# New step orders on all five engines of a gated cross-attention block with routed FFN

## The reference

```python
def xattn(x, y):                                     # x: layernormed
    q = heads(x @ wq + bq); k = heads(y @ wk + bk); v = heads(y @ wv + bv)
    attn = softmax(einsum('bhqd,bhkd->bhqk', q, k) / sqrt(16))
    return merge(einsum('bhqk,bhkd->bhqd', attn, v)) @ wo + bo

def ffn(x):                                          # x: layernormed, 2048 x 256
    one_hot = onehot(argmax(softmax(x @ gate_w.T)), 2)
    h = relu(einsum('end,edh->enh', x[None] * one_hot.T[:, :, None], w1) + b1[:, None])
    expert_out = einsum('enh,ehd->end', h, w2) + b2[:, None]
    return expert_out.sum(0) + relu(x @ sw1 + sb1) @ sw2 + sb2

x = x + tanh(g_xattn) * xattn(layernorm(x), ctx)
x = x + tanh(g_ffn) * ffn(layernorm(x))
```

## Time and profile before

| | |
|---|---|
| runs | 337.96, 338.2, 340.09 us |
| median | 338.2 us |
| profiled execution | 339.18 us, of it span of the trace 337.4 us |
| TensorE busy | 317.1 us, 94% |
| VectorE, ScalarE, GpSimd busy | 232.3 (69%), 214.6 (64%), 186.2 (55%) us |

### The profile page before, as it was taken

One profiled execution on the slowest core, in us unless ns is written; L12 is line 12 of the kernel. 1 busy time (PEld: TensorE's weight loads), 2 busy tenths in 40 slices (PEclk: granted clock), 3 DMA queues, 4 the chain that ended last, 5 costly groups with the idle time before them and its releaser, 6 DMA issues.

```text
span 337.4 us, 7289 instructions
## 1 busy us (share of the span) xinstructions
PE 317.1 (94%) x2363; PEld 281.4 (83%) x2363; DVE 232.3 (69%) x517; ACT 214.6 (64%) x483; POOL 186.2 (55%) x261
## 2 busy tenths in 40 slices
...
GB/s 195 285 353 40 246 124 161 70 171 157 81 82 54 0 126 0 0 144 122 20 230 2 62 2 31 128 63 180 179 64 200 187 62 62 78 61 54 91 31 28
DMA packets 38151, 35.69 MB, mean 106 GB/s; under 512 B 16608, under 2 KB 35060, under 8 KB 37613
## 3 DMA queue, kind: packets, MB, share of 16 engines
...
...
## 4 chain that ended last, share of the span: by engine, by line
PE 64%; DVE 15%; ACT 7%; DMA 6%; issue 4%; POOL 1%; POOLq 1%; SPq 1%; ACTq 0%; DVEq 0%
PE y_ps L1545 24%; PE h_ps L1545 17%; PE bank L1545 9%; PE s_ps L1545 8%; DMA x_all<-in_x 5%; PE bank L1678 3%; DVE rsum L1267 2%; DVE smax L1249 2%; DVE probs L1261 1%; ACT probs L950 1%; DVE stats L1150 1%; ACT xn L901 1%; ACT pT L959 1%; DVE other_sum L1235 1%; PE bank L1782 1%
## 5 line engine op out<-in xcount | busy, mean ns | idle before, releaser
L693 POOL TENSOR_TENSOR probs<-probs,rinv 128x616 f32<-128x616 f32 x32 | 41.3, 1292 | 36.5 <-DVE rinv L1271 35.9
L1545 PE MATMUL y_ps<-sw,hT_hi 128*128 128x256 f32 x272 | 57.2, 291 | 1.2 <-DVE hT_lo L1523 1.2
L1545 PE MATMUL y_ps<-ew,hT_hi 128*128 128x256 f32 x256 | 54.6, 287 | 1.7 <-DVE hT_lo L1482 1.7
L1482 DVE TENSOR_TENSOR hT_lo<-h,hT_hi 128x256 fp32r<-128x256 f32 x64 | 28.9, 451 | 35.0 <-ACT h L1089 33.0
L1545 PEld LDWEIGHTS y_ps<-sw,hT_hi 128*128 128x128 f32 x272 | 44.9, 190 | 3.0 <-DVE hT_lo L1523 1.8
L1545 PEld LDWEIGHTS y_ps<-ew,hT_hi 128*128 128x128 f32 x256 | 42.7, 188 | 3.0 <-DVE hT_lo L1482 2.8
L1545 PE MATMUL h_ps<-x2T_hi,sw 128*128 128x512 f32 (+1 forms) x160 | 43.7, 359 | 0.0
L1086 ACT ACTIVATE hT_hi<-h_ps,vec_cols 128x256 fp32r<-128x256 f32 x32 | 15.2, 475 | 42.0 <-PE h_ps L1545 32.1
L998 ACT ACTIVATE hT_hi<-h_ps,vec_cols 128x512 fp32r<-128x512 f32 (+1 forms) x40 | 24.6, 614 | 22.5 <-PE h_ps L1545 18.0
L1545 PE MATMUL y_ps<-sw,hT_lo 128*128 128x256 f32 x136 | 38.4, 282 | 0.0
L1545 PE MATMUL y_ps<-ew,hT_lo 128*128 128x256 f32 x128 | 35.9, 281 | 0.0
...
## 6 DMA issues: line engine op xcount, KB each, us to landing
...
xs<-sorted_dram SPq DMA_DIRECT2D x8, 257.0 KB, 2.7
...
```

The costliest lines, as they stand in the source:

```text
L693: nc.gpsimd.tensor_tensor(pq, pq, rinv[:, b % 2, k, :].unsqueeze(2).to_broadcast([P, HG, KEYS]), ALU.mult).then_inc(p_ready, 1)
L1482: nc.vector.tensor_tensor(hT[1][:, c % HB, 0:RTOK], h32[:, c % 2, 0:RTOK], hT[0][:, c % HB, 0:RTOK], ALU.subtract).then_inc(h_lo, 1)
L1545: return nc.tensor.matmul(out_, lhsT, rhs, start=start, stop=stop, **kw)
```

## The change

Only the five tables change. Every step occurs as often as before, no function is touched, and each engine executes the same instructions in another order. After the change the line numbers are lower by one, as `PE_ORDER` is a line shorter. The digits for the banks are new as well. Of the diff the part of SP is short enough to be read as it is:

```diff
 SP_ORDER = """
-    fl.0 kw.0 vz.0 vz.1 kw.1 kr.1 kr.2 wd.0 vw.0 wd.1 vw.1 vr.0 kr.3 vw.2 vr.1 vr.2 kr.4 vw.3 wd.3 vw.4 vr.3
-    kr.5 vr.4 wd.2 vw.5 vw.6 vr.5 kr.6 vw.7 ps.0 kr.7 vr.6 vr.7 ps.1 wd.4 wd.5 ps.2 ps.3 xs
+    kw.0 kw.1 vz.0 vz.1 kr.1 wd.0 vw.0 wd.1 kr.2 vr.0 vw.1 kr.3 vr.1 vw.2 kr.4 wd.3 vr.2 vw.3 vr.3 kr.5 vw.4 kr.6
+    vr.4 wd.2 vw.5 kr.7 vr.5 vw.6 vw.7 vr.6 vr.7 wd.4 wd.5 ps.0 ps.1 xs ps.2 ps.3 fl.0
 """
```

More of the change, by code:

```diff
@@ L92 @@
[L92 to L96, removed]
+    warm.0 yt.0 yt.1 yt.2 yt.3 vt warm.1 kp.0.0 in.0.0 kp.0.1 kp.1.0 qy.0.0 kp.1.1 sc.0.0 in.1.1 vp.0 qy.1.1 vp.1
@@ new lines @@
+    ine.5.0 qe.4 ex.3.0 vae.1.1 te.2.0.0 te.2.1.0 xn2.0 q32.5.0 te.2.2.1 te.2.3.0 te.2.4.1 n2e.0.0.0 qe.5 ex.3.1
+    ex.3.2 vae.2.1 he.0 te.3.0.0 ex.3.3 nm.6 he.1 he.2 te.3.1.1 he.3 ine.6.0 ex.4.0 he.4 te.3.2.1 he.5 nm.7 te.3.3.0
+    te.3.4.1 he.6 ex.4.1 q32.6.0 ine.7.1 he.7 xn2.1 vae.3.0 n2e.1.0.1 ex.4.2 n2e.1.1.0 ex.4.3 he.8 qe.6 ex.5.0 he.9
+    he.10 he.11 te.4.0.1 te.4.1.0 te.4.2.0 te.4.3.1 he.12 te.4.4.0 ex.5.1 ex.5.2 q32.7.1 vae.4.0 he.13 ex.5.3
+    te.5.0.0 qe.7 ex.6.0 ex.6.1 te.5.1.0 he.14 te.5.2.1 te.5.3.1 te.5.4.1 he.15 ex.6.2 ex.6.3 xn2.2 vae.5.0
@@ L112 @@
+    n2e.2.0.1 ex.7.0 n2e.2.1.0 ex.7.1 te.6.0.1 te.6.1.0 he.16 he.17 te.6.2.1 te.6.3.1 ex.7.2 te.6.4.1 he.18 wh.2
+    he.19 vae.6.1 ex.7.3 te.7.0.1 te.7.1.0 he.20 wh.3 he.21 he.22 te.7.2.0 te.7.3.1 xn2.3 te.7.4.1 he.23 n2e.3.0.0
+    n2e.3.1.1 vae.7.0 he.24 he.25 he.26 he.27 wh.5 wh.4 he.28 he.29 xn2.4 n2e.4.0.0 he.30 he.31 he.32 he.33 he.34
+    he.35 he.36 he.37 othe.0 he.38 he.39 xse.1
 """
@@ new lines @@
+    r1.1.12 wolo sm.0.0 ss.0.0 inl.1.1 su.0.0 s1.2 s1.3 s1.4 s1.5 s1.6 s1.7 sd sm.0.1 ss.0.1 sm.0.2 su.0.1 sm.0.3
+    ss.0.3 su.0.2 sm.1.0 sm.1.1 inl.2.0 su.0.3 ss.1.1 su.1.0 su.1.1 sm.1.2 sm.1.3 ss.1.2 ss.1.3 inl.3.0 su.1.2
+    sm.2.0 ss.2.0 su.1.3 sm.2.1 su.2.0 ss.2.1 inl.4.1 val.0.0 sm.2.2 ss.2.2 x1.0.0 sm.2.3 su.2.1 wl.1 sm.3.0 s2.0
+    inl.5.0 su.2.2 su.2.3 val.1.1 sm.3.1 su.3.0 ss.3.1 x1.1.1 dg sm.3.2 ss.3.2 wl.0 n2l.0.0.0 su.3.1 su.3.2 sm.3.3
+    ss.3.3 val.2.1 sm.4.0 hl.0 su.3.3 x1.2.0 hl.2 inl.6.0 s2.1 hl.3 ch.0 sm.4.1 ss.4.1 su.4.0 sm.4.2 ss.4.2 hl.6
@@ L128 @@
+    hl.26 hl.27 ot.1.0 x1.7.0 s2.4 pl.3.0 ch.4 n2l.4.0.0 wl.5 hl.30 hl.31 pl.4.1 ot.1.1 ad.3 hl.32 wl.4 hl.34 hl.35
+    seam hl.38 hl.39 ids xsl.1 ad.4
 """
 POOL_ORDER = """
[L130 to L132 removed]
```

71 lines of the change are left out of this document (29 added, 42 removed).

## The result

The changed kernel took 336.99 us (median of 20 runs, 334.6 to 340.19), the kernel before 338.63 (20 runs, 337.31 to 341.92). The ratio is 0.9936 with a 95% interval of 0.9908 to 0.9964: 0.64% faster, 2.2 us, where 4.0 us were forecast. The profiled execution took 335.66 us (span 333.9), so the two profiled executions lie 3.5 us apart, the medians only 1.6. That gap between trace and median is what the experiments are about. The clocks of the 20 runs hint at its source: seven of the changed kernel have a mean granted clock of TensorE of 0.994 or more and take 335.6 us in the mean, the other thirteen lie at 0.979 to 0.990 and take 338.0.

The account below looks back on a forecast made before the run. TensorE bounds the kernel from h.0.0 (76 us) on, with idle time in small waits ahead of it. Terms 1 to 4 (−4.5), 5 (−0.5) and 6 (+1.0) sum to −4.0: 339.18 becomes 335.2, 334.2 against the median; range 331.5 to 338.5.

Parts of the forecast that it names:

- term 1: First root refinement on VectorE, freed from colliding with GpSimd: 0.8 of the 1.18 us wait at sc.0.3 comes back.
- term 2: in.2.0 placed ahead of tn.0, directly behind sc.1.1 on TensorE: qy.2 comes earlier, worth 1.55 us.
- Term 4: Second layernorm's first root ro.0 in one piece on GpSimd, wl.1 ahead of its seeds: 0.9 us earlier at h.0.0.
- Term 3, the clock: qy.2.1 on TensorE back at full instead of half clock, as the pause ahead becomes short: 1.3 us won.
- The rival on late keys: Batch 2's keys kr.2 land late behind weight loads on SP, delaying sc.2.0: +1.05 us, 335.3; chance 0.17.
- The rival on the clock: TensorE still idles ahead of qy.2 and the clock falls anyway, losing term 3: 335.5 us; chance 0.13.
- Terms 5 and 6: Behind h.0.0: 0.5 us of TensorE idle time won; at the hand-over to the loop 1.0 us lost waiting for the remainder.
- the fill as a rival: fl.0, last on SP, might land late for the loop's second tile; held covered, sharing 0.16 with late GpSimd.

Follow-up runs that it names:

- e15: Kernel before, filled with idle-time matmuls, with only the weight split wl.1 moved ahead of the root's seed s2.0 on VectorE; h.0.0 at 76.16 us, 65.52 behind in.0.
- e4: Changed kernel with only the weight split wl.1 put back behind the root's seed s2.0 on VectorE; ratio to the kernel before 0.9957.
- e1: All five tables as in the changed kernel up to h.0.0, as in the kernel before from there on; ratio to the kernel before 0.9997.
- e5: The changed kernel run again unaltered; ratio to the kernel before 0.9886.
- e8: As e3, with batch 1's keys kr.1 also ahead of the zeroing transfer vz.1 on SP; ratio to the kernel before 0.9827.
- e10: The changed kernel unaltered, as a control on another chip; ratio to the kernel before 0.9891.
- e3: Changed kernel with xst three y steps earlier, seam directly behind hl.32, wl.4 behind hl.35, fl.0 behind vr.7; ratio to the kernel before 0.9833, median 333.51 us.
- e6: The changed kernel unaltered, a third trace; span 334.2 us, h.0.0 at 72.42.
- e11: Kernel before with four, five and eight idle-time matmuls in TensorE's pauses ahead of sc.0.3, sc.1.0 and qy.2.1; ratio to the kernel before 0.9988.
- e14: Changed kernel with nine idle-time matmuls ahead of sc.1.0, in.2 put back behind tn.0 and its copy behind te.0.1; sc.1.0 to qy.2 5.89 us instead of 3.29.

## Why the prediction was wrong, by its own steps

**Terms 1, 2 and 4** were too small in sum. In executions without a fall of the clock `h.0.0` comes 61.5 us behind `in.0` in the new order and 65.4 to 65.5 in the old: 3.9 to 4.0 us, where these terms were given 3.25. One by one, term 1 (0.8) measured 0.65 to 1.1; term 2 (1.55) measured 2.6 at `qy.2`. Term 4 (0.9) rested on the root in one piece, which appears in the trace just as told; but freed by itself in the old order it brought nothing (e15), and what the split's place is worth in the new one, 1.9 (e4), runs through VectorE's queue. The terms overlap and aren't additive.

**Term 3, the clock, is the step that failed.** It took the half clock of the earlier trace rows for a property of the old order that the new one sheds, and valued it at `qy.2`'s own delay, 1.3. Both halves were wrong. The stall comes and goes between executions of one program. To the old order it cost 0.5 to 0.6 us at `h.0.0` in the profiled execution, since the engines behind set the pace. And "the long pause ahead of it becomes a short one" missed where the pause went: `kr.1` now stands behind both `vz` on SP, and `sc.1.0` waits 2.3 to 2.6 us. The rival on late keys watched `kr.2` and forgot `kr.1`. In the new order the clock fell behind that pause in four of the eight traces whose early lists are the new ones without fill (e1, e5, e8 and e10; not in the first, e3, e4, e6) for about 7 us, and cost 1.9 to 2.2. The rival on the clock had the right mechanism, but looked for it ahead of `qy.2`, and priced it as the 1.3 not gained (335.5), where a fall behind the new pause takes about 2 from what is gained elsewhere.

**Luck.** `h.0.0` was forecast at 71.7 and measured 71.75. That is two errors that cancel: 3.9 to 4.0 for 3.25, and 0.5 for the 1.3 of the clock. And it holds for a trace without a fall only.

With a fall in half of the executions the new order loses about 1 us in the mean; the old one, with none, one and two stretches in its three traces without fill, some 0.6. So the quiet gain of 3.9 becomes about 3.5 where 4.5 was forecast.

**Terms 5 and 6** were forecast at −0.5 and +1.0, together +0.5 from `h.0.0` to the loop. The traces of the new order take 0.05 to 0.8 us longer than the first of before (149.80) there, which agrees in sum, again with two errors: TensorE's idle time up to `xst` fell from 1.33 to about 0.3 us, 1.0 instead of 0.5, and at the hand-over the wait for the remainder is 1.04 as worked out, but the register reads were left out, 0.4 to 1.1 more. The loop, forecast as unchanged, waits 2.1 us at its first tile in some executions (the first trace, e4 and e6), 0.6 to 1.2 in others; in the rows of the first the late `fl.0` stands behind it. That was half seen (the fill as a rival, by its landing), but the chain runs over SP's later store and GpSimd's first gather. e3, which mends the remainder and `fl.0` (the register reads stay), is 4.1 us shorter in span than the first trace after.

The sum for the profiled pair was therefore good, −4.0 for −3.5, and the step from it to the medians was not: both profiled executions were taken as typical. The one of before was 0.6 us above its median and had a fall of the clock, the one of after 1.3 us below its own and had none. Put together, the mended terms give 2.7 to 3.5 us, and 2.2 was measured. That rest is open: two other comparisons of the same pair give 1.1%, the first 0.64%, with intervals that overlap, and the clock also falls at other places in some executions (in the loop in e4). Nor is it known why e11's median lies 2.3 us above its fastest execution with clocks that are all high; a late start is a candidate (e10 and e14 began 2 and 3 us late), no trace of e11 shows it.
